# Softmax values summed two blocks after the exponentials, and the two maxima pairs of a block apart: a gated cross-attention and mixture-of-experts layer on one Trainium2 core

## The reference

```python
x = x + tanh(g_xattn) * attention(layernorm(x), ctx)     # x, ctx: 32 batches of 128 x 512
x = x + tanh(g_ffn) * moe(layernorm(x))                  # router, top 2 of 8 experts, a shared expert

def attention(x1, x2):                                   # 128 channels, 512 positions, 8 heads of 16
    q, k, v = proj(x1T, Wq, bq), proj(x2T, Wk, bk), proj(x2T, Wv, bv)
    scores = einsum('bhqd,bhkd->bhqk', q, k) / sqrt(16)
    out = einsum('bhqk,bhkd->bhqd', softmax(scores, axis=-1), v)
```

## Time and profile before

| | |
|---|---|
| median of the runs shown | 1448.16 us |
| the profiled execution's own time | 1446.75 us |
| its span in the profile | 1444.9 us |
| PE busy | 1319.2 us (91%) |
| DVE busy | 889.8 us (62%) |
| ACT busy | 853.4 us (59%) |
| POOL busy | 730.8 us (51%) |

### The profile page before, as it was taken

The page is one execution under the profiler, slowest core; times in us unless marked ns, Lnnn a source line. Parts: engine busy times, 40 slices in busy tenths (PEclk is TensorE's granted clock), DMA queues, the critical chain, the costliest instruction groups (busy, mean ns, idle before and its releaser), DMA issues.

```text
span 1444.9 us, 27029 instructions
## 1 busy us (share of the span) xinstructions
PE 1319.2 (91%) x9190; PEld 716.7 (50%) x9190; DVE 889.8 (62%) x1176; ACT 853.4 (59%) x1684; POOL 730.8 (51%) x978
## 2 busy tenths in 40 slices
PE   5989998998998998899999988899899999999997
PEld 2333333333333333333333333387678888888886
DVE  6777777777777778877777776256554333333332
ACT  1677777777777777777777776533234433333332
POOL 7445555545555555546776552120732555555553
PEclk7899999999999999999999998699999999999999
DMA  6555455545545544544665651164963898786665
GB/s 177 151 125 171 149 135 152 156 134 146 162 134 142 163 134 141 169 126 119 148 157 122 140 124 47 64 208 139 105 165 91 190 216 211 180 195 113 109 111 81
DMA packets 123841, 205.84 MB, mean 142 GB/s; under 512 B 28005, under 2 KB 29676, under 8 KB 123710
## 3 DMA queue, kind: packets, MB, share of 16 engines
q1 hardware_dynamic: 105454, 166.74, 42.9%
q0 software_dynamic: 18256, 37.38, 14.1%
HBM read 82.34 MB, written 61.94 MB: 100 GB/s over the span
## 4 chain that ended last, share of the span: by engine, by line
PE 72%; issue 9%; ACT 8%; DVE 4%; DMA 4%; POOL 2%; POOLq 1%; SPq 0%; ACTq 0%; DVEq 0%
PE m_banks L933 20%; PE bank L890 18%; PE bank L860 14%; PE m_banks L838 9%; ACT arena L1351 4%; PE bank L815 4%; PE bank L865 3%; DVE row_max L1089 2%; DMA arena<-ht_d 2%; PE bank L821 2%; ACT arena L1366 2%; POOL xs L757 1%; PE bank L955 1%; PE bank L877 1%; DMA out<-xs,arena 1%
## 5 line engine op out<-in xcount | busy, mean ns | idle before, releaser
L1089 DVE TENSOR_REDUCE row_max<-m_banks 128x2 f32<-128x1024 f32 x512 | 605.9, 1216 | 181.9 <-PE m_banks L838 181.0
L1351 ACT ACTIVATE arena<-bank 128x512 f32<-128x512 f32 x1024 | 557.1, 598 | 227.4 <-PE bank L860 226.5
L890 PE MATMUL bank<-arena 128*32 128x512 f32 x2048 | 284.0, 627 | 70.0 <-ACT arena L1366 68.8
L860 PE MATMUL bank<-q_stack,k_stack 49*128 49x512 f32 x1024 | 285.4, 472 | 2.2 <-ACT arena L1351 2.0
L860 PEld LDWEIGHTS bank<-q_stack,k_stack 49*128 49x128 f32 x1024 | 123.4, 189 | 277.9 <-issue 162.5
L838 PE MATMUL m_banks<-k_stack,q_stack 48*128 48x512 f32 x1024 | 195.9, 456 | 7.3 <-DVE row_max L1089 7.2
L769 POOL DMA_INDIRECT out<-xs,arena x71 | 112.6, 1586 | 159.8 <-ACT xs L1429 121.8
L933 PE MATMUL m_banks<-w_ring,h_hi 128*128 x568 | 183.1, 403 | 0.0
L1418 ACT ACTIVATE arena<-m_banks 128x256 f32<-128x256 f32 x103 | 39.5, 384 | 183.3 <-PE m_banks L933 183.3
L838 PEld LDWEIGHTS m_banks<-k_stack,q_stack 48*128 48x128 f32 x1024 | 90.2, 191 | 98.5 <-issue 68.0
L890 PEld LDWEIGHTS bank<-arena 128*32 128x32 f32 x2048 | 42.6, 109 | 156.2 <-ACT arena L1351 114.3
(11 more groups left out here) (175 smaller groups left out, 1795.0 us busy)
## 6 DMA issues: line engine op xcount, KB each, us to landing
k_stack<-arena SPq DMA_DIRECT2D x192, 128.0 KB
q_stack<-arena SPq DMA_DIRECT2D x192, 128.0 KB
split_d<-staged SPq DMA_DIRECT2D x30, 512.0 KB, 5.1
w_ring<-split_d SPq DMA_DIRECT2D x60, 256.0 KB
arena<-in_w SPq DMA_DIRECT2D x36, 256.0 KB, 7.5
arena<-in_ctx SPq DMA_DIRECT2D x32, 256.0 KB, 3.2
xs<-in_x SPq DMA_DIRECT2D x32, 256.0 KB, 4.0
arena<-arena SPq DMA_DIRECT2D x64, 128.0 KB, 3.2
```

The costliest lines, as they stand in the source:

```text
L860: nc.tensor.matmul(out, k_stack[b % 3][rows, h, kt * P:(kt + 1) * P], q_stack[b % 3][rows, h, :], start=True, stop=True).then_inc(s_es, 1)
L890: last = nc.tensor.matmul(pv_ps[2 * DH * j:2 * DH * (j + 1), :], v_ones[b % 3][:, kt, GROUP * g + j, :], probs[pair % 3][:, j, :], start=( ...
L1089: nc.vector.reduce_max(pair, m_ps[(STEPS * b + u) // 2 % M_PAIRS], AX_X).then_inc(s_mx, 1)
L1351: nc.scalar.activation(probs[group % 3][:, j, :], bank_of["scores", b, s], ACT.Exp, scale=float(DH) ** -0.5).then_inc(s_exp, 1)
```

## The change

PE's loop over the blocks puts only one pair of maxima scores ahead of each pair of scores (ahead of steps 4k and 4k+1, and ahead of 4k+2 and 4k+3) instead of both at the block's start. The values of a block come two blocks behind its exponentials instead of one. To match, ACT's copy of the values bank moves two steps back, behind the exponentials of steps 6 and 22 (`VALUES_LATE` 5); the token turn moves from block 3 to block 1, the logits from block 4 to block 2, the projection of the values from block 2 to block 3, DVE's reciprocal from step 12 to 14, and on SP the sending of the maxima row goes ahead of the sending of the denominators. No instruction is added or left out.

```diff
@@ -32,15 +32,15 @@
 COLUMNS = tuple(slice(c, c + 2 * DH) for c in range(0, P, 2 * DH))
 STEPS = HEADS * KT
 
-PROJECT_AT = {24: (3, 0), 28: (3, 1), 8: (2, 2)}
-EVAC_AT = {27: (3, 0), 31: (3, 1), 11: (2, 2)}
+PROJECT_AT = {24: (3, 0), 28: (3, 1), 12: (2, 2)}
+EVAC_AT = {27: (3, 0), 31: (3, 1), 15: (2, 2)}
 MAX_AT = (19, 3)
-VALUES_LATE = 3
-TURN_TOKENS_AT = 12
-LOGITS_AT = 16
+VALUES_LATE = 5
+TURN_TOKENS_AT = 4
+LOGITS_AT = 8
 MOMENTS2_AT = 10
 MOMENTS_AT = 27
-RECIP_AT = 12
+RECIP_AT = 14
 GROUP = 4
 EXPERTS = 8
 FF = 256
@@ -501,10 +501,10 @@
             for i in TURNS:
                 if is_b(i + 2):
                     copy_parts(i + 2, 0, HI)
+                if is_b(i):
+                    row(i, 1)
                 if is_b(i - 1):
                     spread_denominators(i - 1)
-                if is_b(i):
-                    row(i, 1)
                 if is_b(i + 2):
                     copy_parts(i + 2, 0, LOW)
                 if is_b(i - 1):
@@ -970,14 +970,15 @@
                 for s in range(0, STEPS, GROUP):
                     if is_b(i + 1):
                         max_scores(i + 1, s)
-                        max_scores(i + 1, s + 2)
                     if is_b(i):
                         exp_scores(i, s)
                         exp_scores(i, s + 1)
-                    if s == 0 and is_b(i - 1):
-                        values(i - 1, STEPS // GROUP - 1)
-                    if s and is_b(i):
-                        values(i, s // GROUP - 1)
+                    if s < 2 * GROUP and is_b(i - 1):
+                        values(i - 1, STEPS // GROUP - 2 + s // GROUP)
+                    if s >= 2 * GROUP and is_b(i):
+                        values(i, s // GROUP - 2)
+                    if is_b(i + 1):
+                        max_scores(i + 1, s + 2)
                     if is_b(i):
                         exp_scores(i, s + 2)
                         exp_scores(i, s + 3)
@@ -996,7 +997,8 @@
                     if i == B - 1 and s == FIRST_JOB_AT:
                         gate_up(0)
 
-            values(B - 1, STEPS // GROUP - 1)
+            for r in range(STEPS // GROUP - 2, STEPS // GROUP):
+                values(B - 1, r)
 
             for j in range(JOBS + 1):
                 if j in ROUTER_JOBS:
```

## The result

The changed kernel takes 1410.39 us (median of 4 runs, 1408.73 to 1417.43) against 1448.93 us for the kernel before (4 runs, 1446.69 to 1449.96): ratio 0.9745, 95% interval 0.9709 to 0.9781, 38.5 us less. The prediction was 1432 us with a range of 1422 to 1447: the right side, and outside the range.

A forecast was written before the change was run, and what follows sets the result against it. PE was taken as the engine to follow, standing about 2.6 us per 27.30 us turn, mainly waiting for ACT's copy. 1446.75 - 16 = 1430.8 us; the shown runs' median lies 1.4 higher, so 1432, range 1422 to 1447.

The forecast's parts named there:

- What goes: On PE, the values' waits of 0.99 + 1.25 us go, except in block 5; so does 0.36 ahead of logits.
- what comes in its place: Three rotating score banks now pace most blocks, mostly 3.33 us; the turn takes 26.77 us against 27.30.
- The unknown price: On PE, one maxima pair alone between values and scores; scores behind it taken at 0.33, exponential 0.44 us behind.
- ring and wait cancel: Late second scores and projection blocks on PE cost 0.55 us a turn: no change, 1448 us; 11%.
- the lone maxima pair is no cover: Scores behind a lone maxima pair act as behind values: 0.5 us a turn more than before, 1463 us; 8%.
- the ring of three banks: Score banks in rotation: the second score waits for a freed bank, starting at S + 1.58 us in most blocks.
- It holds for some 30 turns. 30 x 0.53 = 16 us: In the attention, the steady turn's gain of 0.53 us was counted for 30 turns, 16 us in all.
- The clock, the other way: Half-clock spells mid-attention go with the long waits; two turns give back 3 us each: 1426 us; 12%.
- The clock: More numerous small PE waits bring six more half-clock turns, costing 18 us: 1450 us, slower or the same; 7%.
- The cover of what moved back: SP's copies and the reciprocal move back about 1.7 us at no cost; POOL has 13 us free a turn.

The follow-up runs named there:

- b: The changed kernel with both maxima pairs together at the block's start again; 1382.6 us, ratio 0.958 to the kernel before.
- c: The kernel before with only the maxima pairs set apart; 1555.4 us, ratio 1.079.
- j: The changed kernel with ACT's copy of the values bank two exponentials later; 1502.0 us, ratio 1.037 to the kernel before.
- m: The changed kernel with the copy two exponentials later and four unused products ahead of each wait for it; 1473.5 us, ratio 1.020 to the kernel before.
- a: The kernel before with four unused products ahead of each wait of the values for the copy; 1435.1 us, ratio 0.992.
- e: The kernel before with ACT's copy of the values bank one exponential earlier; 1385.3 us, ratio 0.959.
- h: The kernel before with four unused products ahead of the waits for the copy in turn 31 alone; 1446.5 us, ratio 1.000.
- l: The kernel before with four unused products ahead of the waits for the copy in turns 30 and 31; 1480.3 us beside 1485.8, ratio 0.997.
- g: The changed kernel with maxima pairs together, copy one exponential earlier, token turn, logits and values' projection in blocks 3, 4, 5; 1360.8 us, ratio 0.941 to the kernel before.
- d: The kernel before with only the extra pieces (values' projection, token turn, logits) moved; 1438.5 us, ratio 0.996.
- i: The changed kernel with ACT's copy of the values bank one exponential later; 1450.7 us beside 1485.8, ratio 0.979 to the kernel before.

## Why the prediction was wrong

**"What goes" and "what comes in its place": right, to a few hundredths.** Of the eight blocks summed at 3.33, 3.80, 3.33, 3.33, 3.33, 2.99, 3.33, 3.33 none is off by more than 0.02. The unknown price, one maxima pair alone between values and scores, was 0.34 before the scores (413.12 to 413.46), and the scores behind it cost 0.33 to the next piece (413.46 to 413.79), as taken. The rivals "ring and wait cancel" and "the lone maxima pair is no cover" fell by these two rows. b and c confirm that the ring of three banks sets the pace where the second maxima pair doesn't cover it; the turns expected of the twelve other kernels are right within 0.3 us, most within 0.1.

**"It holds for some 30 turns. 30 x 0.53 = 16 us": the step that failed.** As a sum over steady turns it is right (turns 3 to 17: 7.7 measured, 8.0 forecast). As the total it left out the turns that aren't steady. The clock was put at nothing in this sum. I left turn 31 out of the count, since it has no maxima, and took the turns 0 to 2 for like the rest or less. Turn 31 gave 9.3 us, the first three 5.4, the turns 18 to 22 9.4.

**"The clock, the other way" (12%, 1426): right in mechanism, mis-sized.** I priced it from the one slow turn that I had put into the earlier trace rows, two turns at 3 us. The clock record of the kernel before had 54.6 us of low clock in the attention, 24 of them in turn 31, and at 0.46 us each they were worth about 25 us, not 6. With the windows of the last turn (clock 0.65) at hand this case would have read 1446.75 + 1.4 - 16 - 25 = 1407, with all the low clock gone; 1410.4 came, with 6.8 us left. That nearly all of it would go could not be read from the kernel before. The term that was mis-sized is thus the clock's: 0 in the forecast and 6 in the rival, where 47.8 us of low clock went, worth some 22. That the low clock comes from PE standing is shown by j against m (150.2 and 13.7 us with the same order), supported by the places of the 59 spells and by a. That turn 31 lost its time to the clock is shown by e (25.0 us in nearly the old order); which waits set that spell off is not: filling those for the copy in turn 31 alone (h) did nothing, filling turn 30 too (l) went with a turn of 26.1 us.

**"The clock" (7%, slower): fell here**, but c and j show that its mechanism is real and its price larger than I gave, up to 80 us.

**The cover of what moved back** held: the experts part takes the same time (514.2 and 514.6 us), and POOL is 14.09 us busy in a turn as before. With no bank more the kernel gained 6% (g), by the order of the work around the ring alone. The rule of the Trainium skill ("Perfetto Trace Analysis", Optimization Strategy), that a repeated gap can mean too few buffers, fits the ring, for which PE waits 20.6 us in 69 waits in the changed kernel; but no kernel with a bank more was run, and the gain here needed none.

What stays open: why one wait is followed by a spell and the next is not. The length of a wait doesn't decide it (before and c have the same waits of 0.98 to 1.26 us, and 54.6 against 235.5 us of low clock), nor does the time that PE stands in a turn (2.6 us before, 2.3 in j, and j has nearly three times the low clock). Between runs of one kernel on one chip it varies as well: those of the kernel before had mean clocks from 0.964 to 0.981 in the set of e, g, h and j.

## What to carry to other kernels

A wait's length isn't its price when the engine is TensorE: list where the granted clock falls, turn by turn and in the first and last ones too, before multiplying a steady turn's gain by a count. A wait on a copy out of a shared bank is first of all a matter of the copy's place in its engine's order: here one number, one exponential earlier, gained more than a restructuring with three more edits. And when work is spread to fill one wait, ask what it was covering where it stood; the second maxima pair had covered the reuse of a score bank.

## What the runs showed of the hardware

Waits of 0.98 to 1.26 us for the copy, on a PE that is some 90% busy (89% in c, 92% in j), were enough for spells at 1.2 GHz. In the turns 3 to 29 of the kernel before, c, d, h and j they last 3.4 to 10 us; the longest in the last turns are 24 us (before), 27 (h) and 58 (j). Each of the 59 in the turns 3 to 29 began around the end of such a wait, but only about one such wait in five was followed by one. Waits of up to 0.6 us for the copy (i, e) brought none in the turns 3 to 28. Four products of no use put into each such wait gave back 28 us net in m against j (24 by the ratios).

Two scores in different row halves of the array that start together take 0.40 us, as long as a lone one (430.62 and 431.10 in the changed kernel). When the second starts late the gain is gone: at 429.94 in the kernel before it started 0.37 us behind, and the two took 0.87 us.
